# List blocks at other places of a round, a third slot for gathered rows, and rounds written out

## The chip, the cores and the metric

One core of one Trainium2 chip runs the whole program. The metric is the device time of one execution in microseconds. TensorE (PE) is the matrix engine, with its weight loads (PEld) beside it; VectorE (DVE), ScalarE (ACT) and GpSimd (POOL) are the others; SyncE (SP) only issues transfers.

## The reference

A graph of 6250 nodes with 128 features and 200,000 edges, given by `src` and `dst`; the edges are sorted by `dst`, and `dst` is about 6250 u^2, so low nodes have many edges and high ones few. With h = relu(layernorm(x)):

```
x = x + relu([h, sum over edges of h[src] at dst, sum of edge_attr at dst] @ W.T + b)
h = relu(layernorm(x))
h = relu(mean over edges of h[src] at dst @ W1_l + b1 + h @ W1_r)
x = x + relu(mean over edges of h[src] at dst @ W2_l + b2 + h @ W2_r)
```

The sums over edges of node features occur three times, once per layer. All else is small.

## The kernel before

The nodes are cut into 49 blocks of 128. A first part (to about 670 us) reads the edges once, sums `edge_attr` per node, and builds, for the 39 lower blocks ("dense" blocks, `DENSE`), a table of counts: how many edges go from each node to each node of the block. It is stored in DRAM as `counts[b]`, 784 KB a block in 8-bit numbers. The change leaves this part alone.

Then come three rounds, one per layer. The nodes' rows (already multiplied by the layer's weights, split into a high and a low half of 16 bits) lie in SBUF as `G`, and in DRAM as `g_rows[r]`. A round goes through 49 **places**, one block each, in an order that `place_of` gives.

- At a **dense** place TensorE sums 49 matmuls, `stream8[slot]` (the counts of this block) against `G` (L1044). SP loads `counts[b]` into a ring of four slots.
- Ten blocks (`LISTED`, the ones with the fewest edges) are **list** blocks. Their edges stand in tables of 128 a tile, 18 or 19 tiles in turn (`LIST_TILES`). POOL gathers the source rows of each tile from `g_rows[r]` with one indirect DMA (L826) into a slot of `ring_g`; TensorE multiplies the tiles with one-hot matrices of their targets (`list_hot`, L1075). In round 0 VectorE makes the one-hots of a list three places ahead of it (L1630), and SP stores them as `hot_rows`; in rounds 1 and 2 SP loads them.

Before, lists stand at places 11, 15, 19, ..., 47 (0-based). The ring of gathered rows has two slots, so the gathers of list k wait until list k-2 is summed. In each round POOL may begin when all rows of `g_rows[r]` are stored, that is, when the round before has ended.

VectorE takes the sums of each place (L1596, L1599) as `summed` rises, and in rounds 0 and 1 makes with ScalarE the next h of the block. One place later TensorE turns it (L1056) and multiplies it with the next weights (L1062), ScalarE and VectorE write the new `G` (L1250, L1576), and ScalarE stores it to `g_rows[r + 1]`. A list place turns nothing; the place behind it turns two blocks (`to_turn`).

The order on each engine is written out by `one(i, it)`. `whole_round` issues places 0 to 7, then a loop (`Fori`) of 5 turns with 8 places each, 3 dense and a list twice over, then place 48. Block numbers, semaphore counts and slots in the loop depend on `it`. Some waits are followed by a `sem_inc` of a semaphore that nobody waits for (`x_seen`, `sums_seen`).

Of the kernel before, what the change touches and what calls it, by code (L numbers as in the profile page):

```python
# [5 lines left out]
P = 128  # L6
# [10 lines left out]
LISTED = 10  # L17
LIST_TILES = (18, 19)
# [36 lines left out]
def message_passing(nc, x, src, dst, edge_attr, L0_W, L0_b, W1_l, b1, W1_r, W2_l, b2, W2_r, out):  # L55
# [30 lines left out]
    assert D == P and BLOCKS % 4 == 1 and LISTED % 2 == 0 and DENSE == 9 + 3 * LISTED and LBLK == 2 and CELLS <= SLOT and DPB % BANKS == 0 and NWIN == HOLDERS * PER and HOLDERS < P  # L86
# [12 lines left out]
    with ExitStack() as ctx:  # L99
# [58 lines left out]
        def half_words(n):  # L158
# [42 lines left out]
        low_i = place(t0 + 9 * D + 240, NDUO).bitcast(I32)  # L201
        high_i = place(t0 + 9 * D + 240 + NDUO, NDUO).bitcast(I32)
        r0 = t0 + 9 * D + 240 + 2 * NDUO
        ring_g = [place(r0 + i * (MOST * GW // 2), MOST * GW // 2).bitcast(F16).rearrange("p (t c) -> p t c", c=GW) for i in range(2)]
        r1 = r0 + 2 * (MOST * GW // 2)
        list_hot_u8 = place(r1, MOST * P // 4).bitcast(U8)
        list_hot = list_hot_u8.bitcast(F8).rearrange("p (t d) -> p t d", d=P)
        list_hot_u8 = list_hot_u8.rearrange("p (t d) -> p t d", d=P)
        assert r1 + MOST * P // 4 <= 24496 and NLIST <= 10 * BLOCKS
# [114 lines left out]
            edge_copied x_seen fin out_stored sums_seen list_hot""".split()}  # L324
        list_landed = [sem(f"list_landed{u}") for u in range(2)]
# [258 lines left out]
        FIRST = 8  # L584
        LOOP = 8
        LOOPS = (BLOCKS - FIRST) // LOOP
        PER_SLOT = [13, 12, 12, 2]
        WORDS = 6
        OUT_STORES = 4 + 4 * LOOPS + 1
# [4 lines left out]
        def place_of(i, it=0, turn=0):  # L594

            if i < FIRST:
                return DENSE - 1 if i == FIRST - 1 else i
            if is_listed(i):
                return it + ((DENSE if i == FIRST + LOOP - 1 else DENSE + LOOPS) + turn)
            return it * 6 + (FIRST - 1 + (i - FIRST) - (i - FIRST) // 4 + turn * 6)  # L600

        def is_listed(i):
            return i >= FIRST and (i - FIRST) % 4 == 3
# [10 lines left out]
        def before(i, it, back):  # L614

            if i < back:
                return place_of(i - back + FIRST + LOOP + 1, LOOPS - 1)
            if i >= FIRST > i - back:
                return place_of(i - back + LOOP, it, -1)
            return place_of(i - back, it)  # L620

        def after(i, it):

            if i == FIRST + LOOP - 1:
                return place_of(FIRST, it, 1)
            return place_of(i + 1, it)

        def whole_round(eng, one, between=None):
            one(0, 0)
            if between is not None:  # L630
                between()
            for i in range(1, FIRST):
                one(i, 0)
            with eng.Fori(0, LOOPS) as it:
                for i in range(FIRST, FIRST + LOOP):
                    one(i, it)
            one(FIRST + LOOP, LOOPS - 1)

        def number(r, i, it):
            return it * LOOP + (i + r * BLOCKS)  # L640

        def slot_of(r, i):
            return (r + i) % 4

        def uses(r, i, it):
            earlier = sum(PER_SLOT[(slot_of(r, i) - q) % 4] for q in range(r))
            return it * (16 * LOOP // 4) + 16 * (earlier + i // 4 + 1)
# [11 lines left out]
        def _(sp):  # L659
# [39 lines left out]
            def rounds():  # L699
                sp.wait_ge(S["group_done"], NGROUP + 4)  # L700
                for r in range(ROUNDS):
                    def one(i, it):
                        if is_listed(i):
                            k = (i - FIRST) // 4
                            hots = hot_rows[bass.ds(it * 2 + k, 1)].rearrange("a p c -> p (a c)")
                            if r == 0:
                                sp.wait_ge(R["list_hot"], it * 2 + (k + 1))
                                sp.sem_inc(R["x_seen"], 1)
                                sp.dma_start(hots, list_hot_u8.rearrange("p t d -> p (t d)")).then_inc(S["hot_stored"], 16)
                            else:  # L710
                                sp.wait_ge(R["summed"], number(r, i, it) + 1)
                                sp.sem_inc(R["x_seen"], 1)
                                sp.dma_start(list_hot_u8.rearrange("p t d -> p (t d)"), hots).then_inc(S["hot_landed"], 16)
                            return
                        slot, b = slot_of(r, i), place_of(i, it)

                        sp.wait_ge(R["summed"], number(r, i, it) + 1)
                        a = counts[b:b + 1] if isinstance(b, int) else counts[bass.ds(b, 1)]
                        sp.dma_start(stream[slot], a.rearrange("b p c -> p (b c)")).then_inc(stream_landed[slot], 16)

                    def all_stored():
                        sp.wait_ge(count_stored[0], 16 * PIECES * (DENSE // 2 + 1))
                        sp.wait_ge(count_stored[1], 16 * PIECES * (DENSE // 2))
                    if r == 0:
                        sp.wait_ge(count_stored[0], 32 * PIECES)
                        sp.wait_ge(count_stored[1], 32 * PIECES)
                        for i in range(4):
                            one(i, 0)
                        all_stored()
                        for i in range(4, FIRST):  # L730
                            one(i, 0)
                        with sp.Fori(0, LOOPS) as it:
                            for i in range(FIRST, FIRST + LOOP):
                                one(i, it)
                        one(FIRST + LOOP, LOOPS - 1)
                    else:
                        whole_round(sp, one)
# [12 lines left out]
        def _(pool):  # L750
# [61 lines left out]
            def rounds():  # L812
                pool.wait_ge(S["edges_ready"], 1)
                pool.wait_ge(S["evacuated"], NDUO)
                for q in range(2):
                    pool.memset(ring_g[q][:, :, 2 * D:GW], 1.0).then_inc(S["ring_ones"], 1)
                pool.wait_ge(S["list_tables"], 2)
                for r in range(ROUNDS):
                    pool.wait_ge(g_stored[r], 16 * (BLOCKS if r > 0 else 1))
                    for k in range(LISTED):  # L820
                        done = r * BLOCKS + FIRST + 4 * k if k >= 2 else r * BLOCKS + 4 * k - 1
                        if k >= 2 or r > 0:
                            pool.wait_ge(R["summed"], done)
                        at = (k // 2 + (LOOPS if k % 2 == 0 else 0)) * MOST
                        for t in range(LIST_TILES[k % 2]):
                            pool.indirect_dma_start(ring_g[k % 2][:, t, 0:2 * D], None, g_rows[r],  # L826
                                                    bass.IndirectOffsetOnAxis(ap=list_src[:, at + t:at + t + 1], axis=0)
                                                    ).then_inc(list_landed[k % 2], 16)
# [11 lines left out]
        def _(pe):  # L840
# [182 lines left out]
            def rounds():  # L1023
# [4 lines left out]
                for r in range(ROUNDS):  # L1028
                    wide = 2 * D + 1 if r == 0 else 2 * D

                    def one(i, it):
# [653 lines left out]
```

## Time and profile before

| | |
|---|---|
| time, median of 3 runs | 1514.26 us (1512.93 to 1514.72) |
| the profiled execution's own time | 1511.41 us |
| its span | 1509.6 us |
| TensorE busy | 1384.2 us (92%) |
| VectorE / ScalarE / POOL busy | 825.2 / 486.0 / 658.6 us |
| mean granted clock of TensorE | 0.977 |

The span is from the first to the last recorded instruction; the time contains what lies around it. Busy is the time in which an engine had an instruction under way. The rounds run from about 675 to 1497 us.

### The profile page before, as it was taken

To read this page: it belongs to the slowest core of one execution; us is meant where nothing else is said; L and a number is where in the kernel's file an instruction comes from. 1 tells how busy PE (TensorE), PEld (TensorE's weight loads), DVE (VectorE), ACT (ScalarE), POOL (GpSimd) and SP (SyncE) were. 2 spreads that over 40 slices of the span, in tenths; PEclk is the share of its full clock that TensorE was granted. 3 is DMA by queue.
4 is the path that set the end of the run, shared out by engine and by line. 5 is a ranking of instruction groups with operands and counts; after the bars stand their busy time and mean duration, and the time that the engine had idled before them with its cause. 6 is when DMAs were issued, how large, how long until landed. Compare 5 with 4: busy or idle time off the path is not lost.

```text
span 1509.6 us, 36666 instructions
## 1 busy us (share of the span) xinstructions
PE 1384.2 (92%) x12165; PEld 1243.5 (82%) x12166; DVE 825.2 (55%) x1839; ACT 486.0 (32%) x1388; POOL 658.6 (44%) x768
## 2 busy tenths in 40 slices
PE   4586999999999999989999988999999899998966
PEld 4455999999999999988888876888888688887855
DVE  6777998888888888853455454422222222221111
ACT  2351123455788888852222322211111010000000
POOL 4301000111121112237177777274777737577772
PEclk9998999999999999999999999999999999999988
DMA  6007678888889898876354655565656656666562
GB/s 173 25 6 198 201 223 233 238 243 252 263 266 265 265 271 266 261 257 189 136 181 150 205 174 161 166 195 165 203 194 207 182 157 211 200 218 200 184 159 62
DMA packets 284676, 294.52 MB, mean 195 GB/s; under 512 B 19414, under 2 KB 250017, under 8 KB 284625
## 3 DMA queue, kind: packets, MB, share of 16 engines
q1 hardware_dynamic: 235541, 213.75, 45.6%
q0 software_dynamic: 26016, 69.24, 16.1%
q10 hardware_dynamic: 23067, 10.89, 2.5%
q8 instruction: 27, 0.44, 0.1%
q14 instruction: 25, 0.20, 0.0%
HBM read 245.70 MB, written 48.11 MB: 195 GB/s over the span
## 4 chain that ended last, share of the span: by engine, by line
PE 55%; POOL 25%; issue 10%; DVE 5%; DMA 2%; ACT 2%; ACTq 0%; DVEq 0%; POOLq 0%
POOL shared L826 25%; PE edge_banks L1008 19%; PE edge_banks L1044 16%; PE banks L982 11%; PE edge_banks L1004 3%; DMA shared<-g_rows,list_src 2%; PE edge_banks L1075 1%; PE banks L919 1%; PE banks L1062 1%; ACT shared L1217 1%; PE edge_banks L851 1%; DVE edge_t L1378 1%; ACT banks L1212 0%; DVE g_even L1448 0%; DVE shared L1329 0%
## 5 line engine op out<-in xcount | busy, mean ns | idle before, releaser
L826 POOL DMA_INDIRECT shared<-g_rows,list_src x555 | 540.8, 974 | 272.2 <-issue 169.9
L1044 PE MATMUL edge_banks<-g_even,shared 128*128 128x257 f16 (+1 forms) x3822 | 446.6, 274 | 5.5 <-DMA shared<-counts 4.6
L1044 PEld LDWEIGHTS edge_banks<-g_even,shared 128*128 128x128 fp8e3 x3822 | 373.6, 98 | 64.7 <-issue 4.8
L1008 PE MATMUL edge_banks<-shared 128*128 128x128 f32 x2744 | 339.9, 276 | 0.0
L1008 PEld LDWEIGHTS edge_banks<-shared 128*128 128x128 f32 x2744 | 323.6, 193 | 0.0
L806 POOL DMA_DIRECT2D counts<-shared x156 | 76.5, 491 | 460.4 <-ACT shared L1217 442.0
L1596 DVE SCALAR_TENSOR_TENSOR shared<-edge_banks,shared,own 128x128 f32<-128x128 f32 x98 | 34.4, 351 | 384.9 <-PE edge_banks L1044 335.1
L1044 PE MATMUL edge_banks<-shared 128*128 128x256 f16 x1911 | 225.8, 272 | 0.9 <-DVE own L1578 0.9
L1522 DVE TENSOR_TENSOR shared<-iota,shared 128x3528 f16<-128x3528 f16 x98 | 195.4, 1994 | 47.2 <-PE banks L982 46.8
L1217 ACT ACTIVATE shared<-banks 128x392 uint16<-128x392 f32 x312 | 152.3, 488 | 187.6 <-PE banks L982 178.5
L1044 PEld LDWEIGHTS edge_banks<-shared 128*128 128x128 fp8e3 x1911 | 185.3, 97 | 31.4 <-DVE own L1578 1.2
L982 PE MATMUL banks<-shared 128*128 128x196 f16 x1764 | 187.0, 250 | 17.7 <-issue 6.8
L982 PEld LDWEIGHTS banks<-shared 128*128 128x128 f16 x1764 | 162.7, 142 | 29.1 <-issue 17.8
L1212 ACT ACTIVATE banks<-zeros 128x392 f32<-128x392 f16 x312 | 156.1, 500 | 28.6
L1530 DVE TENSOR_TENSOR shared<-shared 128x2304 f16<-128x2304 f16 x98 | 132.4, 1351 | 0.0
L1075 PE MATMUL edge_banks<-shared 128*128 128x256 f16 (+1 forms) x555 | 77.6, 297 | 37.8 <-DMA shared<-g_rows,list_src 37.7
L1075 PEld LDWEIGHTS edge_banks<-shared 128*128 128x128 fp8e3 x555 | 58.0, 106 | 51.6 <-issue 40.1
L1004 PE MATMUL edge_banks<-shared 128*128 128x128 f32 x392 | 83.2, 294 | 0.4
L1244 ACT ACTIVATE shared<-banks 128x128 f32<-128x128 f32 x98 | 27.2, 278 | 169.1 <-PE banks L1056 166.2
L1594 DVE TENSOR_SCALAR shared<-edge_banks 128x1 f32 (+1 forms) x49 | 7.7, 158 | 126.0 <-PE edge_banks L1044 113.6
L1505 DVE TENSOR_TENSOR edge_t<-edge_t,edge_banks 128x128 f32 x200 | 56.8, 284 | 21.3 <-PE edge_banks L1008 7.2
L1537 DVE TENSOR_TENSOR shared<-iota,shared 128x512 f32<-128x512 f16 x98 | 67.0, 684 | 0.0
(276 smaller groups left out, 1012.1 us busy)
## 6 DMA issues: line engine op xcount, KB each, us to landing
shared<-in_edge_attr SPq DMA_DIRECT2D x195, 512.0 KB, 4.6
shared<-counts SPq DMA_DIRECT2D x117, 784.0 KB
counts<-shared POOLq DMA_DIRECT2D x156, 196.0 KB, 4.0
shared<-g_rows,list_src POOLq DMA_INDIRECT x555
shared<-hot_rows SPq DMA_DIRECT2D x20, 304.0 KB
g_rows<-g_even SPq DMA_DIRECT2D x1, 3136.0 KB, 15.1
g_rows<-shared ACTq DMA_DIRECT2D x49, 64.0 KB
g_rows<-g_even ACTq DMA_DIRECT2D x49, 64.0 KB
```

Source lines behind the costliest of these rows:

```text
L806: pool.dma_start(to[k * rows:(k + 1) * rows], stage[s][k * rows:(k + 1) * rows]).then_inc(count_stored[s], 16)
L826: pool.indirect_dma_start(ring_g[k % 2][:, t, 0:2 * D], None, g_rows[r], bass.IndirectOffsetOnAxis(ap=list_src[:, at + t:at + t + 1], axis ...
L982: pe.matmul(all_slots[:, bass.ds(at[s], CELLS)], hot_lo[u][:, :, n], hot_cell[u][:, n, :], start=False, stop=True, skip_group_check=True). ...
L1004: pe.matmul(edge_ps[bank], ring[:, bank * GROUP_TILES, :], hot_dst[u][:, k, FIRST_HOT:GROUP_HOT], start=True, stop=True, skip_group_check= ...
L1008: mm = pe.matmul(edge_wide[bank][:, :, at], ring[:, bank * GROUP_TILES + j, :], hot_dst[u][:, k, (j - 1) * SPREAD:j * SPREAD].unsqueeze(1) ...
L1044: mm = pe.matmul(acc[s][:, 0:wide], stream8[slot][:, order[h], :], G[r % 2][:, order[h], 0:wide], start=h == 0, stop=h == BLOCKS - 1, skip ...
L1075: mm = pe.matmul(acc[s][:, 0:wide], list_hot[:, t, :], ring_g[k][:, t, 0:wide], start=t == 0, stop=t == tiles - 1, skip_group_check=True)
L1212: act.activation(duo[j % BANKS], zeros16[:, 0:1].unsqueeze(1).broadcast_to([P, DUO, CELLS]), ACT.Copy).then_inc(S["zeroed"], 2)
L1217: act.activation(stage_duo[s][:, :, j * WIN:(j + 1) * WIN].rearrange("p h (w d) -> p h w d", w=DUO), duo[j % BANKS].rearrange("p w (d h) - ...
L1522: dve.tensor_tensor(hot_cell[u][:, 0:n, :].rearrange("p s (c k) -> p s c k", k=2), iota16[:, 0:CELLS].rearrange("p (c k) -> p c k", k=2).u ...
L1530: dve.tensor_tensor(hot_lo[u][:, :, 0:n].rearrange("p (a b) s -> p a b s", b=LO_B), hot_a[:, :, mine].unsqueeze(2).broadcast_to([P, LO_A, ...
L1537: dve.tensor_tensor(hot_dst[u][:, :, 0:GROUP_TILES * SPREAD].rearrange("p k (j c) -> p k j c", c=SPREAD), iota16[:, 0:REACH].unsqueeze(1). ...
```

## The change

Rounds are written out in full: `whole_round` and the loops over `it` go, and every engine issues places 0 to 48 one by one with constant block numbers and semaphore values. `LIST_AT` gives the places of the ten lists, and any engine asks `is_listed(i)`. The ring of gathered rows has three slots. Dense blocks take the four slots of `stream` in the order of their use, no matter what lists lie between. The `sem_inc`s of `x_seen` and `sums_seen` go. SP stores the one-hots of a list at the place after it. To make room, two tables of the final check (`low_i`, `high_i`) move to where h lay. Which blocks are lists, and the order of the lists, are unchanged.

```diff
+LIST_AT = (6, 11, 15, 20, 25, 29, 34, 38, 43, 47)
+RING = 3
...
-        ring_g = [place(r0 + i * (MOST * GW // 2), ...) for i in range(2)]
+        ring_g = [place(r1 + i * (MOST * GW // 2), ...) for i in range(RING)]
...
-        def turns_none(i):
-            return i >= FIRST - 1 and (i - FIRST) % 4 == 3
+        def is_listed(i):
+            return i in LIST_AT
+        def list_of(k):
+            return k // 2 + (0 if k % 2 else LISTED // 2)
+        def place_of(i):
+            return DENSE + list_of(LIST_AT.index(i)) if is_listed(i) else DENSE_AT.index(i)
...
-            return () if turns_none(i) else (2, 1) if turns_none(i - 1) else (1,)
+            return () if is_listed(i) else (2, 1) if is_listed(i - 1) else (1,)
...
+        def stream_use(r, i):
+            return r * DENSE + DENSE_AT.index(i)
+        def list_use(r, k):
+            return r * LISTED + k
+        def done_at(n):
+            return n + 5
...
+                        if i > 0 and r == 0 and is_listed(i - 1):
+                            k = LIST_AT.index(i - 1)
+                            sp.wait_ge(R["list_hot"], k + 1)
+                            sp.dma_start(hot_rows[k], list_hot_u8...).then_inc(S["hot_stored"], 16)
                         if is_listed(i):
+                            if r > 0:
+                                last = number(r, LIST_AT[k - 1]) if k > 0 else number(r - 1, LIST_AT[-1])
+                                sp.wait_ge(R["summed"], done_at(max(last, n - 4)))
+                                sp.dma_start(list_hot_u8..., hot_rows[k]).then_inc(S["hot_landed"], 16)
                             return
-                        sp.wait_ge(R["summed"], number(r, i, it) + 1)
+                        g = stream_use(r, i)
+                        if g >= 4:
+                            sp.wait_ge(R["summed"], done_at(number_of_use(g - 4)))
+                        sp.dma_start(stream[g % 4], counts[place_of(i)]).then_inc(stream_landed[g % 4], 16)
...
-                        done = r * BLOCKS + FIRST + 4 * k if k >= 2 else r * BLOCKS + 4 * k - 1
-                        if k >= 2 or r > 0:
-                            pool.wait_ge(R["summed"], done)
+                        use = list_use(r, k)
+                        if use >= RING:
+                            old = use - RING
+                            pool.wait_ge(R["summed"], done_at(number(old // LISTED, LIST_AT[old % LISTED])))
                         for t in range(LIST_TILES[k % 2]):
-                            pool.indirect_dma_start(ring_g[k % 2][:, t, 0:2 * D], ...)
+                            pool.indirect_dma_start(ring_g[use % RING][:, t, 0:2 * D], ...)
...
-                    whole_round(dve, one, check_sums if r == 2 else None)
+                    for i in range(BLOCKS):
+                        if r == 2 and i == 1:
+                            check_sums()
+                        one(i)
```

## Rows read from the trace of the kernel before

**Rows 1.** Windows: busy us and count by engine, clock, DMA share, GB/s; rounds 0, 1, 2.

```profile
675.00:969.00 294.00, 281.44 (x2342) 237.10 (x2343) 140.15 (x488) 80.02 (x240) 189.12 (x183) 0.98 0.53 174
969.00:1237.00 268.00, 259.99 (x2250) 224.68 (x2248) 72.24 (x258) 32.71 (x102) 174.84 (x185) 0.99 0.60 186
1237.00:1497.00 260.00, 237.85 (x2095) 205.57 (x2093) 53.23 (x163) 0.65 (x2) 174.83 (x185) 0.96 0.60 183
```

**Rows 2.** Waits of TensorE in rounds 0, 1, 2: total us, times, longest.

```profile
PE edge_banks L1075 <- DMA shared<-g_rows,list_src: 10.3, 3, 4.1
PE edge_banks L1075 <- DMA shared<-g_rows,list_src: 7.1, 1, 7.1
PE edge_banks L1075 <- DMA shared<-g_rows,list_src: 20.3, 4, 7.5
```

**Rows 3.** Timeline of TensorE, list blocks: start us, us, instructions, idle before.

```profile
1136.99 2.26 PE L1075 MATMUL edge_banks<-shared 128*128 128x256 f16 x19
...
1157.44 2.15 PE L1075 MATMUL edge_banks<-shared 128*128 128x256 f16 x18
...
1177.79 2.25 PE L1075 MATMUL edge_banks<-shared 128*128 128x256 f16 x19
...
1205.51 3.85 PE L1075 MATMUL edge_banks<-shared 128*128 128x256 f16 x18 [7.11 <-DMA shared<-g_rows,list_src]
...
1394.87 4.21 PE L1075 MATMUL edge_banks<-shared 128*128 128x256 f16 x19 [6.07 <-DMA shared<-g_rows,list_src]
...
1468.66 3.69 PE L1075 MATMUL edge_banks<-shared 128*128 128x256 f16 x18 [7.49 <-DMA shared<-g_rows,list_src]
```

**Rows 4.** Windows: the stretch behind the wait of round 1.

```profile
1205.50:1209.30 3.80, 3.79 (x19) 2.67 (x20) 0.00 (x0) 0.00 (x0) 2.87 (x4) 0.53 0.21 54
```

**Rows 5.** Gathers on POOL: all; grouped (busy, mean ns, idle) in two stretches; timeline.

```profile
L826 POOL DMA_INDIRECT shared<-g_rows,list_src x555: 940/945/3348, 672.4 to 1483.9; - x185
L826 POOL DMA_INDIRECT shared<-g_rows,list_src x148 | 156.1, 1054 | 76.7 <-issue 46.2 <-PE edge_banks L1075 30.4
L826 POOL DMA_INDIRECT shared<-g_rows,list_src x148 | 139.9, 945 | 54.2 <-issue 45.1 <-PE edge_banks L1075 8.9 <-PE edge_banks L1044 0.3
...
1244.80 0.94 POOL L826 DMA_INDIRECT shared<-g_rows,list_src  x1 [22.10 <-DMA g_rows<-g_even]
...
1391.38 0.94 POOL L826 DMA_INDIRECT shared<-g_rows,list_src  x1 [0.30 <-issue]
...
1460.14 0.95 POOL L826 DMA_INDIRECT shared<-g_rows,list_src  x1 [0.31 <-issue]
```

**Rows 6.** Timeline of VectorE: L1599, one per place, just behind its sums.

```profile
684.07 0.35 DVE L1599 SCALAR_TENSOR_TENSOR shared<-edge_banks,few,shared 128x128 f32<-128x128 f32 x1
...
690.30 0.35 DVE L1599 SCALAR_TENSOR_TENSOR shared<-edge_banks,few,shared 128x128 f32<-128x128 f32 x1
...
969.29 0.35 DVE L1599 SCALAR_TENSOR_TENSOR shared<-edge_banks,few,shared 128x128 f32<-128x128 f32 x1
...
976.22 0.35 DVE L1599 SCALAR_TENSOR_TENSOR shared<-edge_banks,shared 128x128 f32<-128x128 f32 x1
...
1000.05 0.35 DVE L1599 SCALAR_TENSOR_TENSOR shared<-edge_banks,shared 128x128 f32<-128x128 f32 x1
...
1005.99 0.35 DVE L1599 SCALAR_TENSOR_TENSOR shared<-edge_banks,shared 128x128 f32<-128x128 f32 x1
...
1236.72 0.35 DVE L1599 SCALAR_TENSOR_TENSOR shared<-edge_banks,shared 128x128 f32<-128x128 f32 x1
...
1243.71 0.35 DVE L1599 SCALAR_TENSOR_TENSOR shared<-edge_banks,shared 128x128 f32<-128x128 f32 x1
...
1249.11 0.35 DVE L1599 SCALAR_TENSOR_TENSOR shared<-edge_banks,shared 128x128 f32<-128x128 f32 x1
...
1496.48 0.35 DVE L1599 SCALAR_TENSOR_TENSOR shared<-edge_banks,shared 128x128 f32<-128x128 f32 x1
```

**Rows 7.** DMA queues of 675 to 965 us: packets, MB, share of 16 engines.

```profile
q8 instruction: 7, 0.11, 0.2%
```

More of the change, by code:

```diff
@@ L592, in message_passing @@
         SCHUNKS = -(-SBLK // 4)
[L594 to L600, printed above, removed]
[L602 to L606 removed]
+        DENSE_AT = [i for i in range(BLOCKS) if i not in LIST_AT]
+        assert len(LIST_AT) == LISTED and min(LIST_AT) >= 6 and min(b - a for a, b in zip(LIST_AT, LIST_AT[1:])) >= 4 and LIST_AT[-1] == BLOCKS - 2
+        def is_listed(i):
+            return i in LIST_AT
[3 more added lines that the diff above has]
+            return DENSE + list_of(LIST_AT.index(i)) if is_listed(i) else DENSE_AT.index(i)
         def to_turn(i, r):
@@ L611, in to_turn, with before, after, number @@
                 return (1,) if r > 0 else ()
-            return () if turns_none(i) else (2, 1) if turns_none(i - 1) else (1,)
[L614 to L647, printed above, removed]
+            return () if is_listed(i) else (2, 1) if is_listed(i - 1) else (1,)
+        def before(i, back):
+            return place_of((i - back) % BLOCKS)
+        def after(i):
+            return place_of((i + 1) % BLOCKS)
+        def number(r, i):
+            return r * BLOCKS + i
+        def stream_use(r, i):
+            return r * DENSE + DENSE_AT.index(i)
+        def number_of_use(g):
+            return number(g // DENSE, DENSE_AT[g % DENSE])
+        def list_use(r, k):
+            return r * LISTED + k
+        def tiles_landed(r, k):
+            return sum(LIST_TILES[q % LISTED % 2] for q in range(list_use(r, k) % RING, list_use(r, k) + 1, RING))
+        def done_at(n):
+            return n + 5
         def block_at(b):
@@ L726, in rounds @@
                         sp.wait_ge(count_stored[1], 32 * PIECES)
[L727 to L737, printed above, removed]
+                    for i in range(BLOCKS):
+                        if r == 0 and i == 4:
+                            all_stored()
+                        one(i)
                 sp.wait_ge(R["out_stored"], 16 * OUT_STORES)
@@ L814, in rounds @@
                 pool.wait_ge(S["evacuated"], NDUO)
-                for q in range(2):
+                for q in range(RING):
                     pool.memset(ring_g[q][:, :, 2 * D:GW], 1.0).then_inc(S["ring_ones"], 1)
@@ L1029, in rounds, with one @@
                     wide = 2 * D + 1 if r == 0 else 2 * D
-                    def one(i, it):
-                        n, s, slot = number(r, i, it), (r + i) % 2, slot_of(r, i)
+                    def one(i):
+                        n, s = number(r, i), (r + i) % 2
                         new = r > 0 and i == 0
                         turns = to_turn(i, r) if r < 2 or i == 0 else ()
-                        order = [place_of(k) if k < FIRST else place_of(FIRST + (k - FIRST) % LOOP, (k - FIRST) // LOOP)
-                                 for k in range(BLOCKS)] if new else range(BLOCKS)
+                        order = [place_of(k) for k in range(BLOCKS)] if new else range(BLOCKS)
                         last = BLOCKS - 3 if new else NEAR_END
@@ L1102, in one @@
                         mm.then_inc(R["summed"], 1)
-                    if r == 0:
-                        whole_round(pe, one, lambda: pe.wait_ge(S["zeroed"], 2 * BANKS + 2 * NDUO))
-                    else:
-                        whole_round(pe, one)
+                    for i in range(BLOCKS):
+                        if r == 0 and i == 1:
+                            pe.wait_ge(S["zeroed"], 2 * BANKS + 2 * NDUO)
+                        one(i)
                 pe.wait_ge(S["sums_ready"], 1)
@@ L1264, in store @@
                         def store(back):
-                            b = before(i, it, back)
+                            b = before(i, back)
                             act.wait_ge(R["g_done"], n + 3 - back)
@@ L1280, in one @@
                                 store(1)
-                    whole_round(act, one)
-                    b = place_of(FIRST + LOOP, LOOPS - 1)
+                    for i in range(BLOCKS):
+                        one(i)
+                    b = place_of(BLOCKS - 1)
                     act.wait_ge(R["g_done"], (r + 1) * BLOCKS + 2)
```

140 lines of the change are left out of this document (63 added, 77 removed).

## The prediction

> **What bounds the kernel now.** I read the busy times of the three rounds first, then what TensorE waited for in each, then the two engines' timelines around those waits. From 675 us to 1497 us TensorE is busy 281.4 of 294, 260.0 of 268 and 237.9 of 260 us [rows 1]: it bounds the rounds, and what it is idle is nearly all one kind of wait. In round 0 it waits 10.3 us in 3 waits, in round 1 7.1 us in one, in round 2 20.3 us in four, always L1075 (the sums of a list block) for the gathered rows [rows 2]. After a long wait the first matmuls are slow too: 18 of them take 3.85 us where 18 with no wait take 2.15, and in that stretch the granted clock is 0.53, near the 1.2 GHz level, where a whole round has 0.96 to 0.99 [rows 1, 3, 4]. So a wait costs its length and 1.5 to 2 us more.
>
> Behind the wait stands POOL, which issues the gathers. In round 2, from the first gather of its third list to the last of its tenth, 148 gathers have 139.9 us busy and 45.1 us of issue between them: 1.25 us each [rows 5]. A list of 18 or 19 is 22.5 or 23.75 us. TensorE comes to the next list every four places: in round 1 20.35 us [rows 3], in round 2 3 x 5.40 us and about 2.05 for the list, 18.2 us [rows 3, 6], so POOL loses 3 to 5 us a list. It starts with a lead, as the first list stands at the 12th place, but with two slots it then sits idle until the first list is summed: 30.4 us in round 0, 8.9 in round 2 [rows 5]. The lead is thrown away, and the last lists are late.
>
> **The new places.** List blocks come at 6, 11, 15, 20, 25, 29, 34, 38, 43, 47 (0-based): on average 41/9 = 4.56 places apart. A round computes the same blocks with the same matmuls; nothing is added. What a round costs TensorE without waits: a dense place is 6.23, 5.94 and 5.40 us [rows 6]. Round 0, from the end of place 0 to that of place 48, is 969.29 - 684.07 = 285.2 us; less the 10.3 us of waits and some 1.9 us of slow clock that is 273.0, of which 38 dense places are 236.7, so a list place with its extra turns costs 3.6. Round 1 is 1236.72 - 969.29 = 267.4, less 7.1 and 1.7 = 258.6: place 0 is 6.93 [rows 6], 38 dense 225.7, a list 2.6.
>
> *Round 0.* One step from list to list is on average 3.56 x 6.23 + 3.6 = 25.8 us. POOL has 23.1 us of gathers, and more: the mean gather is 1054 ns here against 945 in round 2, (1054 - 945) x 148 = 16 us over 8 lists, 2.0 us a list [rows 5], where VectorE builds one one-hot per list beside them; POOL is at 25.1 a list. It starts at 672.4 [rows 5]. List 0 has landed by about 672.4 + 22.5 + 2.5 = 697; TensorE wants it at 684.07 + 5 x 6.23 = 715. List 9: 672.4 + 10 x 25.1 + 2.5 = 926 (POOL waits for no slot: list k-3 is always summed by then), wanted at 684.07 + 273 - 10 = 947. Slack is 16 to 20 us: no wait is left. Gain 10.3 + 1.9 = 12.2. Place 7 turned no block and place 8 turned two, around the loop's entry; that pair becomes ordinary, 0.2 us. With the loops' register work and small bubbles on VectorE and ScalarE, on which h of the block before depends, I take 0.7, bounded by 0 and 2. Round 0: 13.1.
>
> *Round 1.* POOL starts about 8.0 us after the end of round 0, as it does after round 1 (1244.80 - 1236.72 = 8.1 [rows 5, 6]); a step of TensorE is 3.56 x 5.94 + 2.6 = 23.8, POOL's is 23.1. List 0: landed at 8.0 + 22.5 + 2.5 = 33.0, wanted at 6.9 + 5 x 5.94 - 0.8 = 35.8 (the last 0.8 is VectorE's delay behind the sums, by which rows 6 are late). The slack of 2.8 grows by 0.7 a list to about 8 at list 9. One landing is late whatever stands before it: list 8 (block 48, the last; I take it that its many padded sources, all one row, do it) is summed 7.6 us after its last gather ends (1460.14 + 0.95 to 1468.66), list 5 only 2.5 us (1391.38 + 0.94 to 1394.87) [rows 3, 5]; 5 us more at list 8 still fit. Gain 7.1 + 1.7 + 0.2 = 9.0.
>
> *Round 2.* Here a step of TensorE is 3.56 x 5.40 + 2.05 = 21.3 us against POOL's 23.1, so POOL bounds the round once its lead is gone. POOL starts 8.1 us after the end of round 1. List by list, TensorE's arrival against the landing, from that end, in us: list 0 33.2 / 33.1; 1 56.8 / 56.6; 2 75.1 / 79.1; 5 about 145 / 149; 7 about 191 / 195.3; 8 219 / 222.8 (its slow landing); 9 241 / 241.6. Five-place steps (23.6 us) catch POOL up by half a microsecond, four-place steps (18.2) wait for 4. I expect waits of 3 to 5 us at lists 2, 5, 7, 8. The slow clock after them mostly eats time in which TensorE would wait for the next list anyway. The sum thus goes by POOL: 8.1 + 185 x 1.25 + 2.5 until list 9 has landed, and 8.1 for list 9 and place 48 (2.25 + 5.4 + VectorE's delay): 249.9 us, against 1496.48 - 1236.72 = 259.8 before [rows 6]. Gain 9.9, of the some 26 that its waits and their clock cost now. Bounds: 8 with a slow clock after list 8 and slower landings, 11 with landings of 1.7 us.
>
> **The third slot.** It removes POOL's wait for a slot. By the sum above, POOL has no such wait in rounds 1 and 2 with the new places even with two slots (list 2 would start after 54 us of round 2, list 0 is summed by 36), and hardly any in round 0 (list 2 at about 721, list 0 summed at 718). I cost it at 0, from 0 to 2 us. One more memset of the ones column is 0.1 us on POOL ahead of a list with 16 us to spare.
>
> **Queues.** SP's loads of dense blocks now wait for the use of four dense blocks ago, not four places ago: never later than before. All of TensorE's waits in rows 2 are for gathered rows, none for such a load, so nothing is gained. The store of a one-hot now is asked for at the place after the list, behind the same comparison as before; the comparison for the next list waits for it two places later, over 12 us against the transfer's few. The loads of one-hots in rounds 1 and 2 keep their lead of four places. ACT's stores of g rows and its order at a list are the same instructions; list 9 and the last place stand as before, so POOL's start in rounds 1 and 2, which waits for the last such store, stays 8 us behind. The output stores run in free time. All 0.
>
> **Rounds written out.** TensorE took 7 packets of 16 KB of instructions in round 0, for 17 written places [rows 7]; 49 places need 20, so 3 rounds have some 40 more. Each takes 0.2% of 16 engines over 290 us, by 7, about 1.3 us, one per 14 us of work: far apart. No wait of TensorE in the written-out places beyond the ones in rows 2 says that it ran dry. The branch back costs it nothing either: from 1136.99 (place 31, the last of a turn of the loop, 19 matmuls) to 1157.44 there is one, from 1157.44 (18 matmuls, 0.11 us less) to 1177.79 none: 20.45 - 0.11 = 20.34 us against 20.35 [rows 3]. I take 0; the removed semaphore increments are hidden the same way.
>
> The Trainium skill, "Runtime: NRT & Kernel Launch", section "Instruction fetch mechanics", says that a taken branch out of the fetched window forces a fetch before execution goes on, and is a reason to unroll. The 20.34 and 20.35 us do not show it here; by the rule 15 branches at a fetch each would go.
>
> **Sum.** 13.1 + 9.0 + 9.9 = 32.0 us. The profiled execution was 1511.41 us (span 1509.6 and 1.8 around it), so the new one would be 1479.4. The median of the timed runs, 1514.26, lies 2.9 above the profiled one: 1482.
>
> **Rivals.**
> *A, little comes from round 2.* Landings get slower as four loads and a gather share the queues, and each of four waits brings its 1.7 us of slow clock: round 2 gains 9.9 - 6, rounds 0 and 1 lose 2. 24 us, 1490. For it: the clock penalty is seen at every wait over 4 us. Against: such time is eaten by the next wait.
> *B, POOL is not the limit of round 2* (the gathers speed up once they are spread): all 20.3 us of waits and 5.7 of clock go; 13.1 + 9.0 + 26 = 48, 1466. Against: 1.25 us a gather, in every round, busy queues or not.
> *C, the branches were paid for* in ways that a timeline of TensorE hides: 15 x 1.3 = 20 us more, 1462. It is the skill's rule as a mechanism; 20.34 against 20.35 speaks against it.
> *D, slower.* TensorE runs dry at each new 16 KB of the written-out code: 40 x 1.3 = 52 us lost against 32 won, 1534. It decides from 0.8 us exposed per packet. Against: the places written out before show no such gap, and the packets come 14 us apart. ScalarE or VectorE, which stand behind TensorE by a place, could run dry for 1 us without harm.
> *E, the places do nothing* as SP or the comparison becomes late in round 0 and eats the gain: 1514.
>
> **Numbers.** Forecast 0.76, A 0.09, B 0.03, C 0.04, D 0.04, E 0.04 (of it half within 0.2%, the rest a little faster or slower). Its own range is 1478 to 1487; with most of A and some room below for round 0 the range is 1474 to 1491. 0.2% is 3 us, about what a measurement can tell from no change. Faster 0.93, same 0.02, slower 0.05.
>
> **What would show it.** No wait of L1075 for gathered rows in rounds 0 and 1; four or more in round 2, of 3 to 5 us, at lists 2, 5, 7, 8, 12 to 18 us in all; POOL with no wait for L1075 over 1 us in any round; round lengths 272, 258.4 and 250 us between the ends that rows 6 give; some 60 instruction packets in the rounds in place of 20. It is wrong if gathers still stall round 1, if POOL's gather is not 1.25 us, or if dense places get longer than 6.23, 5.94 and 5.40 us.

## The result, and the profile after

The changed kernel takes 1470.36 us (median of 4 runs, 1466.89 to 1475.82), the kernel before 1514.49 (1512.93 to 1515.76): a ratio of 0.971, interval 0.9686 to 0.9733. The forecast was 1482, its range 1474 to 1491: right in direction, 12 us too high, and outside its range. The profiled run took 1467.38 us; its span, from the first to the last recorded instruction, is 1465.7.

Where the time went can be read from VectorE's row behind each place's sums (L1599 before [rows 6], L1583 after). The four rows of after are the ends of place 0 of round 0 and of place 48 of rounds 0, 1 and 2:

```profile
681.03 0.35 DVE L1583 SCALAR_TENSOR_TENSOR shared<-edge_banks,few,shared 128x128 f32<-128x128 f32 x1
...
946.19 0.35 DVE L1583 SCALAR_TENSOR_TENSOR shared<-edge_banks,few,shared 128x128 f32<-128x128 f32 x1
...
1205.17 0.35 DVE L1583 SCALAR_TENSOR_TENSOR shared<-edge_banks,shared 128x128 f32<-128x128 f32 x1
...
1454.02 0.35 DVE L1583 SCALAR_TENSOR_TENSOR shared<-edge_banks,shared 128x128 f32<-128x128 f32 x1
```

| us | before | after | difference | forecast |
|---|---|---|---|---|
| until place 0 of round 0 | 684.07 | 681.03 | -3.0 | 0 |
| round 0 | 285.22 | 265.16 | -20.1 | -13.1 |
| round 1 | 267.43 | 258.98 | -8.5 | -9.0 |
| round 2 | 259.76 | 248.85 | -10.9 | -9.9 |
| from there to the end of the span | 13.1 | 11.7 | -1.4 | 0 |

Rounds 1 and 2 came as forecast to within 1 us. Round 0 gave 7 us more. Next come the waits of TensorE for gathered rows in rounds 1 and 2 (total, times, longest; in round 0 there is none), beside [rows 2]:

```profile
PE edge_banks L1059 <- DMA shared<-g_rows,list_src: 0.3, 1, 0.3
...
PE edge_banks L1059 <- DMA shared<-g_rows,list_src: 9.8, 4, 5.0
```

The windows of the three rounds, with the columns of [rows 1], follow: TensorE is busy 286.0 of 290, 251.8 of 253 and 229.2 of 239 us, its clock 0.99, 1.00 and 0.97 (before 0.98, 0.99 and 0.96).

```profile
670.00:960.00 290.00, 285.98 (x2456) 247.35 (x2457) 138.59 (x514) 82.24 (x246) 195.43 (x189) 0.99 0.57 187
960.00:1213.00 253.00, 251.83 (x2193) 218.28 (x2192) 67.11 (x243) 30.97 (x96) 171.54 (x182) 1.00 0.63 194
1213.00:1452.00 239.00, 229.16 (x2023) 198.46 (x2022) 49.38 (x149) 0.00 (x0) 174.62 (x185) 0.97 0.64 195
```

Round 2's list blocks on TensorE stand beside [rows 3]. The list waits that are left stand at lists 1, 2, 6 and 7 (the forecast had 2, 5, 7 and 8), and a long one is still followed by slow matmuls: 19 take 4.21 us behind 5.02 us of waiting, and 2.25 behind 0.61.

```profile
1262.89 2.25 PE L1059 MATMUL edge_banks<-shared 128*128 128x256 f16 x19 [0.61 <-DMA shared<-g_rows,list_src]
1284.88 4.00 PE L1059 MATMUL edge_banks<-shared 128*128 128x256 f16 x18 [3.53 <-DMA shared<-g_rows,list_src]
...
1377.92 2.15 PE L1059 MATMUL edge_banks<-shared 128*128 128x256 f16 x18 [0.67 <-DMA shared<-g_rows,list_src]
1401.30 4.21 PE L1059 MATMUL edge_banks<-shared 128*128 128x256 f16 x19 [5.02 <-DMA shared<-g_rows,list_src]
```

POOL's waits over the rounds: no wait for a slot is over 0.3 us. Before, it stood 30.4 us in round 0 and 8.9 in round 2 [rows 5], and 14.2 in round 1.

```profile
POOL shared L811 <- issue: 168.1, 551, 0.5
...
POOL shared L811 <- PE edge_banks L1059: 0.6, 2, 0.3
```

Round 0 now takes 20 packets of instructions, where [rows 7] had 7, and no gap of TensorE goes with them.

```profile
q8 instruction: 20, 0.33, 0.5%
```

### Where the 7 us of round 0 were

Both kernels have stretches of round 0 in which no list waits for its rows. Lists are counted from 0. Before, TensorE starts the sums of list 1 and of list 5 at these times:

```profile
768.26 1.28 PE L1075 MATMUL edge_banks<-shared 128*128 128x257 f16 x10
...
857.46 1.28 PE L1075 MATMUL edge_banks<-shared 128*128 128x257 f16 x10
```

That is (857.46 - 768.26) / 4 = 22.30 us from list to list, for a list and three dense places. After, a list place and the two places behind it, at list 0, take 712.19 to 727.43 on VectorE, 15.24 us; the same list before took 16.00 (746.88 to 762.88). So these three are 0.76 us shorter, with no wait for a DMA in either. The same sum over the lists 0 to 5, which wait in neither kernel, gives 0.76 to 0.79 each. The last list has only one place behind it in the round and gives 0.34. Nine lists at 0.77 and the last make 7.3 us; for lists 6, 7 and 8, which waited for rows before, the 0.77 is taken over from the others.

```profile
712.19 0.35 DVE L1583 SCALAR_TENSOR_TENSOR shared<-edge_banks,few,shared 128x128 f32<-128x128 f32 x1
714.50 0.35 DVE L1583 SCALAR_TENSOR_TENSOR shared<-edge_banks,few,shared 128x128 f32<-128x128 f32 x1
721.20 0.35 DVE L1583 SCALAR_TENSOR_TENSOR shared<-edge_banks,few,shared 128x128 f32<-128x128 f32 x1
727.43 0.35 DVE L1583 SCALAR_TENSOR_TENSOR shared<-edge_banks,few,shared 128x128 f32<-128x128 f32 x1
```

A list place is short (3.0 us from one row of L1599 to the next, a dense place 6.2), so the place behind it turns the h of a block (L1056) very soon after VectorE has begun on it. Here is the chain before, at the list at 768.26: VectorE takes the sums (L1599), makes x (L1603) and its statistics (L1607, L1610), ScalarE makes h (L1261), and TensorE's weight load of the turn waits 0.42 us for it.

```profile
769.11 0.35 DVE L1599 SCALAR_TENSOR_TENSOR shared<-edge_banks,few,shared 128x128 f32<-128x128 f32 x1
...
769.59 0.29 DVE L1603 SCALAR_TENSOR_TENSOR x_sb<-shared,x_sb 128x128 f32 x1
...
770.03 0.29 DVE L1607 BATCH_NORM_STATS2 shared<-x_sb 128x6 f32 x1
...
770.47 0.18 DVE L1610 BATCH_NORM_AGGREGATE shared<-shared 128x2 f32<-128x6 f32 x1
...
771.66 0.49 ACT L1261 ACTIVATE shared<-x_sb,shared 128x128 f32 x1 [0.67 <-DVE shared L1615]
...
772.20 0.14 PEld L1056 LDWEIGHTS banks<-identz,shared 128*128 128x128 f32 x1 [0.42 <-ACT shared L1261]
```

The same chain after, at the list whose sums start at 760.83:

```profile
761.48 0.35 DVE L1583 SCALAR_TENSOR_TENSOR shared<-edge_banks,few,shared 128x128 f32<-128x128 f32 x1
...
761.87 0.29 DVE L1587 SCALAR_TENSOR_TENSOR x_sb<-shared,x_sb 128x128 f32<-128x128 f32 x1
...
762.19 0.29 DVE L1590 BATCH_NORM_STATS2 shared<-x_sb 128x6 f32<-128x128 f32 x1
...
762.52 0.18 DVE L1592 BATCH_NORM_AGGREGATE shared<-shared 128x2 f32<-128x6 f32 x1
...
763.46 0.49 ACT L1247 ACTIVATE shared<-x_sb,shared 128x128 f32<-128x128 f32 x1 [0.42 <-DVE shared L1597]
...
764.07 0.14 PEld L1040 LDWEIGHTS banks<-identz,shared 128*128 128x128 f32 x1
```

From the start of the list's sums to h it is 771.66 - 768.26 = 3.40 us before and 763.46 - 760.83 = 2.63 after, 0.77 less: 0.20 until VectorE's first row shown, 0.09, 0.12 and 0.11 in its next three steps, and 0.25 from the last of them to h. The waits of TensorE's weight load, which I had not read (my view was that of the matmuls alone, where the wait for h is 1.1 us in 5), show that this chain held TensorE in round 0 before (total, times, longest). The kernel after has none of the three rows.

```profile
PEld banks L1056 <- ACT shared L1261: 5.9, 17, 0.6
...
PEld edge_banks L1051 <- ACT shared L1235: 1.3, 7, 0.2
PE banks L1056 <- ACT shared L1261: 1.1, 5, 0.3
```

### The profile page after: what moved, and what is told of

Read it like the earlier page. It is cut to its first block, busy times and chain, and to the rows that moved or that the text cites. A ratio compares the mean times of both kernels' runs of the same rounds, so it can differ in the third digit from the quotient of the medians.

```text
span 1465.7 us, 34653 instructions
## 1 busy us (share of the span) xinstructions
PE 1373.2 (94%) x12165; PEld 1241.3 (85%) x12166; DVE 815.3 (56%) x1839; ACT 485.5 (33%) x1388; POOL 659.1 (45%) x769
## 4 chain that ended last, share of the span: by engine, by line
PE 75%; POOL 11%; issue 5%; DVE 5%; ACT 2%; DMA 1%; ACTq 0%; DVEq 0%; POOLq 0%
PE edge_banks L1028 31%; PE edge_banks L993 20%; PE banks L967 11%; POOL shared L811 11%; PE edge_banks L1059 3%; PE edge_banks L989 3%; PE banks L1046 3%; PE banks L904 1%; ACT shared L1202 1%; PE edge_banks L1035 1%; PE banks L1040 1%; PE edge_banks L836 1%; DMA shared<-g_rows,list_src 1%; DVE edge_t L1362 1%; ACT banks L1197 1%
## 5 line engine op out<-in xcount | busy, mean ns | idle before, releaser
L1059 PE MATMUL edge_banks<-shared 128*128 128x256 f16 (+1 forms) x555 | 71.7, 282 | 10.1 <-DMA shared<-g_rows,list_src 10.1
L1578 DVE TENSOR_SCALAR shared<-edge_banks 128x1 f32<-128x1 f32 x49 | 7.7, 158 | 131.6 <-PE edge_banks L1028 131.6
```

The lines of the kernel that those rows point to most:

```text
L1059: mm = pe.matmul(acc[s][:, 0:wide], list_hot[:, t, :], ring_g[slot][:, t, 0:wide], start=t == 0, stop=t == tiles - 1, skip_group_check=True)
```

## The experiments

In all kernels below the register values of the first part that ScalarE's and TensorE's waits compare with are held from below at 0 (the bounds, below), by one more instruction on a register each. So each is compared with c0, which is the changed kernel with that and nothing else. The runs stand on several chips, and each ratio is to the kernel before on the same chip; between kernels it is the rounds of the profiled execution that are compared.

**c0, the base.** ScalarE's part of the edit; TensorE's is alike.

```diff
-                act.wait_ge(S["step_done"], regs[j])
+                act.reg_alu(ends[j], regs[j], 0, ALU.max)
+                act.wait_ge(S["step_done"], ends[j])
```

> The changed kernel again, as the base of the experiments: in the part ahead of the rounds, registers loaded from tables are held at 0 or above by one register operation each (8 on ScalarE a block, 8 on TensorE per two steps) before they are waited on; this edit is in every experiment. Both theories: rounds of 265.2, 259.0 and 249 us between the ends of place 0 and place 48 as in the changed kernel; the part before them 0 to 15 us longer. If the start of round 0 varies by 3 us with no edit to the rounds, the 3 us by which it was earlier in the changed kernel are no effect of the change.

Measured: 1477.50 us (1474.94 to 1477.84), ratio 0.9757 [0.9727, 0.9786]. The rounds are those of the changed kernel: 265.16, 258.91, 248.83. The difference to the changed kernel is ahead of them: place 0 ends at 691.5 us against 681.0.

**Four runs on a chip whose TensorE crawled.** On it the kernel before takes 2048.66 us. The cause is open; what it looks like is shown in the last section. f1 is c0 with the old places and two slots, f2 is c0 with two slots, f4 is c0 with the increments back, and cb is the kernel before with the same bounds on its registers. The first three ran again on sound chips, as g1, h2 and g4, where their edits are shown.

> The clamped base with the lists back at places 11, 15, ..., 47 and two slots: only the written-out rounds are left of the change. Theory (the places take the waits for gathered rows away, the written-out code shortens round 0's chain on VectorE and ScalarE by some 0.7 us a list): round 0 about 279 us between the ends of place 0 and place 48, as POOL's 25 us a list now meets a shorter step of 21.5 us and most of the 7 us comes back as waits for gathers; rounds 1 and 2 as before, 267 and 259; 32 us over the base, 1510. Rival 1 (the written-out code is worth nothing, all 44 us come from places and slot): rounds of 285, 267, 259, 1516. Rival 2 (the written-out code is the larger part): under 1495.

> The clamped base with two slots in the ring of gathered rows. Theory (the third slot is idle in effect, since with the new places list k-2 is always summed when POOL comes to list k): rounds as in the base within 1 us each, 1477, with at most 1 us of POOL waiting for a slot per list in round 0. Rival (the third slot carries the gain of the last lists): rounds 1 and 2 get waits again, over 1485.

> The clamped base with the two increments of a semaphore nobody waits for put back on VectorE at each place of round 0. Theory (they were about a third of the shorter chain behind a list, the register-held addresses the rest): round 0 is 1 to 3 us longer than 265.2, at the ten lists only, and waits of TensorE for ScalarE behind a list come back in part. Rival 1 (they are hidden): round 0 within 0.5 us. Rival 2 (they were all of it): 272 us.

> The kernel before with the same clamp. Theory (the 3 us by which round 0 began earlier in the changed kernel are the spread of the part before it; the 1.4 us at the end come with the written-out code): rounds of 285.2, 267.4 and 259.8 us, the end of place 0 between 690 and 695, 13.1 us behind the last place against 11.6. Rival (the part before the rounds is slower in this kernel each time): place 0 ends 3 us later than the base's 691.5.

Measured: 1999.03, 2001.60, 2036.57 and 2049.83 us, ratios 0.9739, 0.976, 0.9942 and 1.0004. Only cb settles something: its interval [0.9988, 1.002] says that the bounds cost at most some 4 us there. Of the others' places and slots the times say nothing, as TensorE crawls through them and POOL stands waiting for slots, mostly 12 to 24 us at a time. How much of each run crawled differs too (TensorE's waits on "issue" at dense places are 280.6 us in cb, 296.3 in f1, 325.4 in f4), so the three aren't compared with one another either.

**g1, written out only.** c0 with the old places and two slots, so that of the change only the loops, the increments and the new order of SP's loads and stores are left.

```diff
-LIST_AT = (6, 11, 15, 20, 25, 29, 34, 38, 43, 47)
-RING = 3
+LIST_AT = (11, 15, 19, 23, 27, 31, 35, 39, 43, 47)
+RING = 2
```

> The clamped base with the lists back at places 11, 15, ..., 47 and two slots, once more, since the run before fell on a chip on which TensorE crawls in stretches whatever the kernel. Theory (the places take the waits for gathered rows away, the written-out code shortens the chain behind a list by 0.7 us): round 0 about 279 us between the ends of place 0 and place 48, as POOL's 25 us a list now meets a shorter step of 21.5 us and most of the 7 us comes back as waits for gathers; rounds 1 and 2 as before, 267 and 259; about 1510. Rival 1 (the written-out code is worth nothing): rounds of 285, 267, 259, 1516. Rival 2 (the written-out code is the larger part): under 1495.

Measured: 1515.34 us against 1514.60 before on the same chip, ratio 1.0012 [0.9998, 1.0027]. Rounds 284.96, 267.52 and 259.53, before 285.22, 267.43 and 259.76. Alone, the written-out code gives nothing: I had expected 279 for round 0, and missed. TensorE's rows say where it went. Its lists 1 to 4 are (835.51 - 770.88) / 3 = 21.54 us apart, 0.76 less than the 22.30 before, so the gain is there in this kernel too. Behind them come two of the lists that wait:

```profile
770.88 1.28 PE L1065 MATMUL edge_banks<-shared 128*128 128x257 f16 x10
...
835.51 1.28 PE L1065 MATMUL edge_banks<-shared 128*128 128x257 f16 x10
...
885.20 2.31 PE L1065 MATMUL edge_banks<-shared 128*128 128x257 f16 x10 [5.29 <-DMA shared<-g_rows,list_src]
...
939.42 2.31 PE L1065 MATMUL edge_banks<-shared 128*128 128x257 f16 x10 [6.59 <-DMA shared<-g_rows,list_src]
```

But POOL starts again only when the slot of list 0 is free. The first gather of list 2 and the last of list 9:

```profile
752.07 0.94 POOL L811 DMA_INDIRECT shared<-g_rows,list_src  x1 [30.37 <-PE edge_banks L1065]
...
953.18 0.94 POOL L811 DMA_INDIRECT shared<-g_rows,list_src  x1 [0.30 <-issue]
```

That is 202.0 us to the end of the last one, and 202.3 before (748.86 to 951.16). It bounds the end of round 0, and what TensorE saves at each list comes back as a wait for the next: 15.3 us in 4 waits, where [rows 2] had 10.3 in 3, and more slow matmuls behind them.

**g4, the increments back.** c0 with the two semaphore increments on VectorE's chain.

```diff
                             dve.wait_ge(R["x_done"], n + 1)
+                            dve.sem_inc(R["x_seen"], 1)
                             dve.bn_stats(bn_blk[:, s, :], a_x).then_inc(R["stats"], 1)
                             dve.wait_ge(R["stats"], n + 1)
+                            dve.sem_inc(R["x_seen"], 1)
                             dve.bn_aggr(agg_blk[:, s, :], bn_blk[:, s, :]).then_inc(R["aggr"], 1)
```

> The clamped base with the two increments put back on VectorE at each place of round 0, once more for the same reason. New theory, from the list places of the crawling chip that were not disturbed (2.53 + 6.59 us for a list and the place behind it, against 2.33 + 6.75): the increments lengthen VectorE's chain by 0.2 us a place but TensorE waits for it only some 0.05 us a list, so round 0 is 265.2 to 266.5 us. Rival (they are a third or more of the 7 us): 267.5 or more.

Measured: 1476.57 us, ratio 0.9745 [0.9719, 0.9771]. Round 0 is 266.06, 0.9 more than in c0. Five kernels without the increments and without a wait for gathers in round 0 have 265.16 or 265.17 (after, c0, h2, h3, f6), so that is clear of the spread. The chain shows the price of each increment: L1599 and L1602, the two statistics, start 0.44 us behind the step before them, and 0.33 in the kernel after.

```profile
769.36 0.29 DVE L1595 SCALAR_TENSOR_TENSOR x_sb<-shared,x_sb 128x128 f32<-128x128 f32 x1
769.80 0.29 DVE L1599 BATCH_NORM_STATS2 shared<-x_sb 128x6 f32<-128x128 f32 x1
770.24 0.18 DVE L1602 BATCH_NORM_AGGREGATE shared<-shared 128x2 f32<-128x6 f32 x1
```

So an increment is 0.11 us, and two are 0.22 of the 0.77 by which h comes sooner. TensorE feels less of it: 0.11 us at every second list, nothing at the others but one, 0.35 at place 38, where the weight load waits 0.41; 0.9 in all. The weight load waits 0.8 us in all, not 5.9. The other 0.55 us of the chain, and some 6.4 of the 7.3 us, are left for the rest of what was written out: constants in place of addresses and counts held in registers, no loop, and no increments on TensorE. That is a difference, not a measurement of its own. The 0.9 is what the increments cost where the chain has slack; with the loops, where TensorE waits for the chain already, they may cost up to 0.22 a list. A kernel with loops and without the increments was not run.

**h2 and h3, the places and the third slot apart.** h2 is c0 with two slots (`RING = 2`), h3 is c0 with the old places and three slots.

> The clamped base with two slots in the ring of gathered rows, once more, since the run before fell on the crawling chip. Theory (with the new places list k-2 is always summed when POOL comes to list k): rounds within 1 us of the base's 265.2, 258.9 and 248.8, POOL waiting at most 1 us for a slot at any list. Rival (the third slot carries the gain of the last lists): waits in rounds 0 and 1 again, 10 us or more in all.

> The clamped base with the lists at places 11, 15, ..., 47 and three slots. Theory (what counts is that POOL never stops in a round; slot or places do it alone, and round 2 is bounded by POOL in both): rounds of 265, 259 and 250 us, waits of 5 and 7 us and 1 to 2 us of slow clock each at the last lists of round 2, 0 to 3 us above the base. Rival (the even spread is what matters): 10 us or more above.

Measured: h2 1480.22 us, ratio 0.9769 [0.9745, 0.9794]; h3 1477.42, ratio 0.9741 [0.9712, 0.977]. Rounds 265.16, 259.01, 250.92 and 265.17, 258.54, 250.34. Either edit alone gives the whole gain of rounds 0 and 1, and neither has a wait for gathers in round 0; with both missing (g1) it is all gone. Both do the same thing, from two sides: the new places free the slots early, the third slot lets POOL go on without them. POOL's waits for a slot in the rounds are 3.4 us in 3 (h2; the longest is 1.7, where I had said 1) and 5.4 us in 1 (h3), where before had 30.4, 14.2 and 8.9.

In round 2, h2 has 2.1 us and h3 1.5 us more than c0, but so has g4 (250.31), which has c0's places and slots. That is the spread of this round between kernels, and the second edit is worth at most the same 1 to 2 us.

**f6, is POOL the limit of round 2?** c0, in which round 2 gathers 12 tiles of each list in place of 18 or 19; the matmuls stay, and multiply rows of earlier lists in place of those not gathered, so a part of the work is left out and the sums are wrong.

```diff
-                        for t in range(LIST_TILES[k % 2]):
+                        for t in range(LIST_TILES[k % 2] if r < 2 else GATHERED):
```

> The clamped base, and in round 2 POOL gathers only the first 12 tiles of each list (the sums then use rows of earlier lists for the rest: that part of the work is left out). Theory (POOL alone bounds round 2, by its start 8 us into the round and 185 gathers of 1.25 us): no wait for gathered rows in round 2, which takes 232.5 us in place of 248.8, rounds 0 and 1 as in the base, 16 us less in all. Rival (the waits of round 2 come from slow landings among the loads of dense blocks): 3 us or less.

Measured: 1455.25 us, ratio 0.9609 [0.9585, 0.9633]. Round 2 is 232.68 us with one wait of 0.4 us in all three rounds:

```profile
PE edge_banks L1066 <- DMA shared<-g_rows,list_src: 0.4, 1, 0.4
```

So POOL holds round 2 back by 248.83 - 232.68 = 16.2 us, and without it the round is what the dense places (6.93 + 38 x 5.40 = 212.1) and ten lists (some 2.05 each) take. The profiled execution of f6 is 23.3 us shorter than that of c0 in all; 3.6 of it lie ahead of the rounds and 3.8 behind them. Why the end is shorter stays open.

**f10, no padded tiles.** The tiles that are gathered follow from the data: blocks 39 to 45 need 18, 46 and 47 need 17, block 48 needs 14. The kernels above gather 18 or 19; the rest are padding, whose sources are all one row. f10 gathers and multiplies only what is needed, and swaps two lists so that block 48 comes first. All of the work is done.

```diff
+TILES_OF = (14, 18, 18, 18, 17, 18, 17, 18, 18, 18)
...
+            k = {0: LISTED - 2, LISTED - 2: 0}.get(k, k)
...
-                        for t in range(LIST_TILES[k % 2]):
+                        for t in range(TILES_OF[k]):
```

> The clamped base with each list given the tiles that its block needs (14 for block 48, 17 or 18 for the others: 174 in place of 185, nothing left out), and the short list of block 48 first in the round in place of ninth. Theory (POOL bounds round 2): POOL has 13.8 us less, TensorE 1.2 us less a round; waits in round 2 fall from 10 to 17 us to about 4, the round from 248.8 to 236 or 238, rounds 0 and 1 by 1.2 each, 13 to 15 us in all. If the slow landing of block 48's list comes from its padded tiles, whose sources are one row, it is gone. Rival (landings): 3 to 5 us.

Measured: 1457.94 us (1457.48 to 1461.38), ratio 0.9631 [0.9605, 0.9657], 19.6 us under c0, where I had said 13 to 15. Rounds 264.26, 257.33 and 234.99 (I had said 236 to 238 for the last): 16.3 us less in all, and 3.4 of the rest lie ahead of them. It beats both kernels. Its waits in all rounds, and the window of round 2, with the clock at 1.00:

```profile
PE edge_banks L1067 <- DMA shared<-g_rows,list_src: 2.9, 2, 1.6
```

```profile
1210.00:1446.00 236.00, 230.43 (x2083) 201.54 (x2081) 53.96 (x168) 0.64 (x2) 164.56 (x174) 1.00 0.63 199
```

All times in us; the first five columns are of the profiled execution, the last is the median of the timed ones.

| | until place 0 | round 0 | round 1 | round 2 | rest | median |
|---|---|---|---|---|---|---|
| before | 684.1 | 285.22 | 267.43 | 259.76 | 13.1 | 1514.49 |
| after | 681.0 | 265.16 | 258.98 | 248.85 | 11.7 | 1470.36 |
| c0, base | 691.5 | 265.16 | 258.91 | 248.83 | 11.7 | 1477.50 |
| g1, written out only | 687.7 | 284.96 | 267.52 | 259.53 | 13.1 | 1515.34 |
| g4, increments back | 688.4 | 266.06 | 259.74 | 250.31 | 11.7 | 1476.57 |
| h2, two slots | 690.9 | 265.16 | 259.01 | 250.92 | 13.1 | 1480.22 |
| h3, old places | 691.2 | 265.17 | 258.54 | 250.34 | 11.7 | 1477.42 |
| f6, 12 gathers in round 2 | 687.9 | 265.16 | 259.13 | 232.68 | 7.8 | 1455.25 |
| f10, tiles as needed | 688.1 | 264.26 | 257.33 | 234.99 | 11.3 | 1457.94 |

## Why the prediction was off, step by step

- *What bounds the rounds, and why POOL is late.* Right. POOL's gathers kept their 1.25 us, the lead was thrown away at two slots, and f6 shows the bound of round 2 by taking gathers away.
- *Round 0, waits and their clock, 12.2, and places 7 and 8, 0.2.* Right for the first: no wait for gathers is left, and lists 6, 7 and 8 gave 14.6 us, 12.3 of it beyond the 0.77 a list. Places 7, 8 and 9 took 19.2 us in place of 18.7, so that pair gave 0.5. 12.3 + 0.5 + 7.3 = 20.1, the whole of the round.
- *Round 0, "the loops' register work and small bubbles on VectorE and ScalarE, on which h of the block before depends, I take 0.7, bounded by 0 and 2".* This is the term that failed. It measured 7.3 us, 0.77 at each list but the last, over three times the upper bound. The place of it was named right; its size was taken from nothing. The rows for it were in the trace of before: 7.2 us of waits of the weight load for ScalarE in round 0, above. They also speak against the sentence under D that ScalarE and VectorE stand a place behind and could run dry for 1 us without harm: behind a list place TensorE waits for them. And the cost of a list place with its turns, 3.6 us in the prediction, held that wait and was carried over to the new kernel; there it is 15.24 - 2 x 6.23 = 2.8.
- *The removed increments, "hidden the same way", 0.* Not quite: g4 puts them at 0.9 us of round 0, a part of the 7.3.
- *Round 1, 9.0.* 8.5. Right.
- *Round 2, 9.9, by the sum over POOL.* 10.9. The sum was right to 1 us: POOL started 8.0 us after the end of round 1 (1213.17), its 185 gathers took 230.7 us (231.25 forecast), the sums of list 9 began 2.0 us behind them (2.5), and the round was over 8.2 us later (8.1). That so small a difference came out has some luck in it, as TensorE's last wait was at list 7 and at list 9 it came without one. The single waits stood partly at other lists, 9.8 us in all where I said 12 to 18: after the wait and the slow matmuls of list 2 TensorE came to list 5, and after those of list 7 to list 8, with their rows just landed.
- *The third slot, 0.* Right for this kernel, with the new places. Not said in the prediction, and shown by h3: it would have done the places' work without them.
- *Written-out rounds need more packets of code, 0.* Right, 20 packets in round 0 and no gap with them.
- *The rest.* The 3.0 us ahead of the rounds are the same code in both kernels, and the seven kernels with the same first part stand 687.7 to 691.5, so 3.0 is no more than the spread. All seven, which have the bounds, start the rounds later than the two kernels without; what the bounds cost on these chips was not measured. The 1.4 us at the end go with the slots (11.7 with three, 13.1 with two, in the seven kernels but f6 and f10, which change the lists); what of the slots does it stays open.
- *The rivals.* A is refuted by round 2, which gained 10.9 and not 3.9, and B by its waits, which are still there. D's gap is in no row, and E's lost gain neither: round 0 gained 20.1. C, the branches paid in ways that a timeline of TensorE hides, gave 1462 and was nearer in size than the forecast (8 us off, not 12), but its 20 us in all three rounds are not there: round 1, which has hardly a wait left, came 0.5 us longer than a sum with no term for branches. What was hidden was VectorE's and ScalarE's chain in round 0.

In sum: the span is 43.9 us shorter, of which 32.0 were forecast. Of the other 11.9, the mis-sized term is 7.3 - 0.7 = 6.6, what lies outside the rounds 3.0 + 1.4, and the rest of rounds 0, 1 and 2 is +0.4, -0.5 and +1.0.

## What to carry over

Read the waits of the weight loads beside those of the matmuls: a wait that TensorE's matmul row shows as 1.1 us was 7.2 us there. Where two gains meet one bound, as the written-out code and the places do with POOL, neither alone tells its worth: find which engine sets the end of the stretch first, and try the two together and apart. And when gathers bound a stretch, count the tiles that hold nothing: here 11 of 185 a round were padding, and round 2 was 13.8 us shorter without them, more than the 10.9 that the whole change gave it.

## What was not expected of the hardware

**Gathers that all read one row seem to land late.** In before, list 8 of round 2 was summed 7.6 us after its last gather, list 5 only 2.5 [rows 3, 5]. Its last four gathers are padding. In the kernel after, the queue of the gathers takes 92.4% of 16 engines for 5 us behind them, and 10.6 to 26.3% in the three stretches of 5 us before (packets, MB, share; 1406:1411, 1411:1416, 1416:1421 and 1421:1426):

```profile
q0 software_dynamic: 127, 0.26, 22.3%
q0 software_dynamic: 75, 0.16, 10.6%
q0 software_dynamic: 106, 0.19, 26.3%
q0 software_dynamic: 120, 0.27, 92.4%
```

In f10, with block 48's gathers at 962 to 980 us and none of them padding alone, the same queue has no such stretch (970:975, 975:980, 980:985):

```profile
q0 software_dynamic: 64, 0.13, 12.1%
q0 software_dynamic: 160, 0.33, 29.8%
q0 software_dynamic: 128, 0.26, 15.8%
```

The kernel before has the stretch at the same list, 100.9% in 1460:1465. f10 also moves the list to the front of the round, so that the one row is the cause is likely, and not shown by itself.

**A chip on which TensorE crawls.** The four runs above show stretches in which a matmul of 0.37 us comes 0.7 us or more behind the one before (in cb up to 2.9), with "issue" (no wait that the profile shows) between, whatever the kernel. The rows are of cb; the kernel before itself took 2048.66 us there against 1514 elsewhere. No row names a cause.

```profile
1641.30 0.37 PE L1050 MATMUL edge_banks<-g_even,shared 128*128 128x256 f16 x1 [1.73 <-issue]
1642.00 0.37 PE L1050 MATMUL edge_banks<-g_even,shared 128*128 128x256 f16 x1 [0.33 <-issue]
1644.11 0.37 PE L1050 MATMUL edge_banks<-g_even,shared 128*128 128x256 f16 x1 [1.73 <-issue]
```
